# GpSimd writes ones on the diagonal of the residual's low part; the correction's product with the unit matrix goes

## What is computed

```python
def step(Sst, inp):
    q_t, k_t, v_t, g_t, beta_t = inp
    Sst = Sst * jnp.exp(g_t)[..., None, None]
    kv = jnp.einsum('bhk,bhkv->bhv', k_t, Sst)
    delta = (v_t - kv) * beta_t[..., None]
    Sst = Sst + k_t[..., None] * delta[:, :, None, :]
    o = jnp.einsum('bhk,bhkv->bhv', q_t, Sst)
    return (Sst, o)
```

## Time and profile before

| | |
|---|---|
| median of 3 runs | 1304.82 us (1302.67 to 1306.89) |
| the profiled execution | 1303.8 us, its span 1302.0 us |
| PE busy | 1200.0 us, 92% of the span |
| DVE busy | 1131.6 us, 87% |
| ACT busy | 975.0 us, 75% |
| POOL busy | 663.9 us, 51% |

### The profile page before, as it was taken

The page is one execution under the profiler, slowest core; times in us unless marked ns, Lnnn a source line. Parts: engine busy times, 40 slices in busy tenths (PEclk is TensorE's granted clock), DMA queues, the critical chain, the costliest instruction groups (busy, mean ns, idle before and its releaser), DMA issues.

```text
span 1302.0 us, 35596 instructions
## 1 busy us (share of the span) xinstructions
PE 1200.0 (92%) x13356; PEld 1008.6 (77%) x13356; DVE 1131.6 (87%) x2092; ACT 975.0 (75%) x2076; POOL 663.9 (51%) x566
## 2 busy tenths in 40 slices
...
GB/s 131 1 18 2 26 50 27 42 34 35 31 50 38 43 47 34 54 26 54 26 54 26 42 26 42 27 42 26 66 2 42 10 203 162 291 67 120 118 69 100
DMA packets 123893, 75.10 MB, mean 58 GB/s; under 512 B 93272, under 2 KB 116324, under 8 KB 122192
## 3 DMA queue, kind: packets, MB, share of 16 engines
...
...
## 4 chain that ended last, share of the span: by engine, by line
PE 79%; DVE 11%; issue 3%; ACT 2%; POOL 2%; DMA 2%; SPq 0%; POOLq 0%; DVEq 0%; ACTq 0%
PE bank L559 12%; PE bank L714 6%; PE bank L701 5%; PE bank L760 5%; PE bank L731 4%; PE bank L749 4%; PE bank L740 4%; PE bank L649 3%; PE bank L641 3%; PE bank L657 3%; DVE con L1056 2%; PE bank L609 2%; PE bank L610 2%; PE bank L1657 2%; PE bank L1682 2%
## 5 line engine op out<-in xcount | busy, mean ns | idle before, releaser
L1056 DVE SCALAR_TENSOR_TENSOR con<-bank,taps,con 128x1022 f32<-128x1022 f32 (+2 forms) x192 | 245.3, 1278 | 21.3 <-ACT con L829 16.7
L1214 POOL TENSOR_TENSOR gl<-const_sb,gc 128x512 f16<-128x512 f32 x128 | 130.0, 1043 | 120.7 <-DVE gc L1066 75.7
L559 PE MATMUL bank<-x,qkv 128*128 128x512 f16 x768 | 184.6, 392 | 6.4 <-DVE con L1056 6.3
L559 PEld LDWEIGHTS bank<-x,qkv 128*128 128x128 f16 x768 | 73.4, 100 | 89.1 <-issue 8.8
L1249 POOL TENSOR_TENSOR oo<-oo 128x512 f16<-128x512 f32 x64 | 76.1, 1199 | 121.8 <-ACT oo L959 121.8
L1114 DVE TENSOR_TENSOR X<-X,bank 128x512 f16<-128x512 f16 x160 | 108.8, 680 | 17.0 <-PE bank L649 15.7
L898 ACT ACTIVATE Z<-bank 128x512 f16<-128x512 f32 x160 | 96.4, 604 | 23.7 <-PE bank L657 23.7
L1105 DVE TENSOR_TENSOR Y<-bank,ymask 128x512 f16<-128x512 f32 x160 | 109.2, 683 | 2.9 <-PE bank L641 2.3
L829 ACT ACTIVATE con<-bank,taps 128x512 f32<-128x512 f32 x128 | 85.4, 687 | 33.1 <-PE bank L559 32.9
L1241 POOL TENSOR_TENSOR kd<-k_tok,gc 128x512 f32<-128x512 f32 x48 | 50.1, 1046 | 111.5 <-PE bank L740 111.5
L760 PE MATMUL bank<-out,sqo 128*128 128x256 f16 x768 | 96.2, 276 | 9.3 <-DMA sqo<-oo 9.2
...
## 6 DMA issues: line engine op xcount, KB each, us to landing
...
```

The costliest lines, as they stand in the source:

```text
L559: last = mm(bank[:, b], qkv16[:, w, a, t * P:(t + 1) * P], x16[:, x, a, b * S:(b + 1) * S], start=(a == k == 0), stop=(a == HT - 1 and k = ...
L1056: stt(out=out, in0=bank[:, 0:B, 0:S - k], scalar=taps[:, par, t, TAPS - 1 - k:TAPS - k], in1=out, op0=ALU.mult, op1=ALU.add).then_inc(tap_ ...
L1214: last = tt(gl[:, g % 2, k].rearrange("p (m r) d -> p m r d", m=2), upper.unsqueeze(1).unsqueeze(1).broadcast_to([P, 2, R, P]), gc[:, par, ...
```

## The change

`Z` loses its fourth product, the unit matrix with Z0 (L690: 4 matmuls a quarter, 16 a head, 256 in all). In its place the low part `res1` gets ones on its diagonal, so that the second product brings in Z0 as well. A new step `one` does that on GpSimd with an affine_select over a quarter (128x512, bf16, in place); it waits for DVE's `res1`, and `Z` on TensorE now waits for it (semaphore `res_low`). A quarter has one such step, so there are 64 more instructions on GpSimd.

```diff
         def finish_z(n, par, g):
 
-            is_free(pe, n, ("res", g), ("once", g), taking=("Z", g))
+            pe.wait_ge(res_low, 4 * n + g + 1)
+            is_free(pe, n, ("once", g), taking=("Z", g))
             out = take(n, "Z", g)
             for j in range(4):
                 u, at = 4 * g + j, slice(j * P, (j + 1) * P)
                 mm(out[:, at], res0[:, g, j], once[:, g % 2, j], start=True, stop=False)
                 mm(out[:, at], res1[:, g, j], Z0[:, u], start=False, stop=False)
-                mm(out[:, at], res0[:, g, j], Z0[:, u], start=False, stop=False)
-                last = mm(out[:, at], ident16[:], Z0[:, u], start=False, stop=True)
+                last = mm(out[:, at], res0[:, g, j], Z0[:, u], start=False, stop=True)
             filled(last, "Z", g)
...
+        def residual_one(n, par, g):
+            is_free(pool, n, ("res", g))
+            nc.gpsimd.affine_select(out=res1[:, g], in_=res1[:, g], pattern=[[0, 4], [1, P]], base=0,
+                                    channel_multiplier=-1, compare_op=ALU.not_equal, fill=1.0)\
+                .then_inc(res_low, 1)
...
-    (0, "solve", 0), (1, "gl", 3), (1, "aH", 1), (1, "decay", 2),
-    (0, "Z", 1), (1, "st", 0), (0, "su", 0), (1, "st", 1),
+    (0, "solve", 0), (0, "one", 1), (0, "one", 2), (1, "gl", 3),
+    (1, "aH", 1), (1, "decay", 2), (0, "Z", 1), (1, "st", 0),
```

More of the change, by code:

```diff
@@ L44 @@
     (0, "once", 1), (0, "res", 3), (1, "aH", 0), (1, "kk", 2),
[8 rows of a table removed]
-    (1, "aH", 3), (2, "load", "qkv"), (1, "turn", (0, 0)), (1, "unit", 3),
[10 rows of a table removed]
[L64 to L81, removed]
+    (0, "solve", 0), (0, "one", 1), (0, "one", 2), (1, "gl", 3),
[4 rows of a table added]
+    (1, "unit", 0), (0, "solve", 1), (0, "once", 3), (1, "p", (0, 0)),
+    (1, "unit", 1), (0, "qs", 1), (1, "st", 2), (1, "aL", 0),
+    (0, "su", 1), (1, "pT", 1), (1, "aL", 1), (1, "y", (1, 0)),
@@ new lines @@
+    (0, "pdl", 1), (1, "unit", 2), (0, "one", 3), (1, "aH", 3),
+    (2, "load", "qkv"), (1, "turn", (0, 0)), (1, "unit", 3), (1, "st", 3),
[10 rows of a table added]
+    (2, "proj", 1), (1, "p", (2, 1)), (1, "load", "out"), (1, "pT", 3),
+    (1, "y", (4, 0)), (0, "solve", 3), (1, "turn", (3, 0)), (2, "tap", 1),
+    (2, "gl", 2), (0, "power", 0), (2, "decay", 0), (1, "y", (3, 1)),
+    (0, "pdl", 3), (1, "p", (4, 0)), (0, "sum", 2), (0, "sum", 3),
+    (0, "sqo", 2), (0, "oT", 2), (2, "silu", 1), (0, "sqo", 3),
+    (1, "turn", (2, 1)), (1, "norm", 0), (2, "proj", 2), (1, "p", (3, 1)),
@@ new lines @@
+    (2, "tap", 2), (2, "sq1", 1), (0, "weigh", 0), (2, "tok", 0),
+    (2, "tok", 1), (1, "turn", (4, 0)), (0, "z", 0), (0, "z", 1),
+    (2, "silu", 2), (0, "high", 0), (0, "z", 2), (0, "low", 0),
+    (0, "low", 1), (0, "oT", 3), (1, "y", (4, 1)), (0, "weigh", 1),
+    (1, "turn", (3, 1)), (2, "proj", 3), (1, "p", (4, 1)), (0, "high", 1),
+    (2, "kT", 0), (0, "z", 3), (2, "kT", 1), (2, "v", (0, 1)),
+    (2, "tap", 3), (1, "turn", (4, 1)), (2, "silu", 3), (2, "v", (0, 0)),
+    (0, "weigh", 2), (0, "weigh", 3), (0, "high", 2), (1, "res", 0),
@@ L82 @@
+    (0, "high", 3), (0, "op", 0), (2, "proj", 0), (1, "once", 0),
+    (2, "tap", 0), (1, "res", 1), (0, "op", 1), (0, "low", 2),
+    (0, "low", 3), (1, "res", 2), (1, "Z", 0), (1, "once", 2),
+    (1, "one", 0), (1, "kd", 1), (2, "silu", 0), (1, "aL", 3),
     (0, "op", 2), (2, "decay", 1), (0, "op", 3),
@@ L136 @@
     (0, "y", (4, 1)), (1, "gl", 2), (1, "tok", 1), (0, "turn", (3, 1)),
[2 rows of a table removed]
+    (1, "proj", 3), (1, "v", (0, 1)), (0, "one", 0), (0, "one", 1),
+    (0, "one", 2), (1, "gl", 3), (0, "p", (4, 1)), (1, "v", (0, 0)),
+    (1, "tap", 3), (0, "one", 3), (1, "pT", 0), (1, "unit", 0),
     (1, "unit", 1), (0, "turn", (4, 0)), (1, "pT", 1), (0, "res", 0),
@@ L180 @@
     (1, "load", "z"), (1, "once", 2), (0, "op", 2), (2, "silu", 0),
-    (2, "decay", 1), (0, "low", 3), (0, "oT", 3), (1, "kd", 1),
-    (0, "op", 3), (1, "pT", 3),
+    (2, "decay", 1), (0, "low", 3), (0, "oT", 3), (1, "one", 0),
+    (1, "kd", 1), (0, "op", 3), (1, "pT", 3),
 ]
 LAST = [
-    (15, "load", "qkv"), (14, "kk", 0), (14, "gl", 3), (14, "load", "out"),
-    (14, "aT", 0), (13, "Z", 2), (14, "kk", 1), (13, "split", "out"),
-    (13, "once", 1), (14, "aT", 1), (13, "res", 3), (13, "solve", 0),
[19 rows of a table removed]
@@ L208 @@
-    (15, "gc", 0), (14, "turn", (1, 1)), (15, "proj", 1), (13, "sum", 1),
[3 rows of a table removed]
[L212 to L217, removed]
@@ L218 @@
-    (13, "high", 0), (15, "silu", 2), (13, "weigh", 1), (15, "tap", 3),
[4 rows of a table removed]
[L223 to L226, removed]
+    (15, "load", "qkv"), (14, "kk", 0), (13, "one", 1), (13, "one", 2),
+    (14, "gl", 3), (14, "load", "out"), (14, "aT", 0), (13, "Z", 2),
@@ new lines @@
+    (14, "kk", 1), (13, "split", "out"), (13, "once", 1), (14, "aT", 1),
+    (13, "res", 3), (13, "solve", 0), (14, "kk", 2), (13, "split", "z"),
[16 rows of a table added]
+    (13, "su", 2), (13, "pdl", 2), (13, "sqo", 2), (14, "load", "z"),
+    (14, "p", (1, 1)), (14, "y", (3, 0)), (14, "turn", (2, 0)), (13, "ks", 3),
+    (13, "qs", 3), (14, "y", (2, 1)), (14, "p", (3, 0)), (15, "gc", 0),
+    (14, "turn", (1, 1)), (15, "proj", 1), (13, "sum", 1), (15, "gl", 0),
+    (14, "aL", 3), (13, "sum", 2), (14, "y", (4, 0)), (14, "p", (2, 1)),
@@ new lines @@
+    (15, "load", "out"), (14, "oT", 0), (14, "kd", 1), (13, "solve", 3),
+    (15, "gl", 1), (15, "tap", 1), (14, "oT", 1), (14, "turn", (3, 0)),
+    (15, "decay", 0), (14, "turn", (2, 1)), (13, "pdl", 3), (15, "silu", 1),
+    (13, "sqo", 3), (14, "norm", 0), (14, "p", (4, 0)), (14, "y", (3, 1)),
+    (15, "proj", 2), (14, "oT", 2), (13, "power", 0), (13, "sum", 3),
+    (14, "p", (3, 1)), (15, "tap", 2), (15, "sq1", 1), (14, "oT", 3),
+    (13, "weigh", 0), (15, "tok", 0), (15, "tok", 1), (14, "turn", (3, 1)),
@@ L227 @@
+    (13, "z", 0), (14, "y", (4, 1)), (13, "z", 1), (13, "high", 0),
+    (15, "silu", 2), (13, "weigh", 1), (15, "tap", 3), (15, "load", "z"),
[4 rows of a table added]
+    (13, "low", 1), (13, "high", 2), (14, "once", 0), (15, "tap", 0),
+    (13, "low", 2), (15, "proj", 0), (13, "high", 3), (15, "silu", 3),
+    (13, "op", 1), (14, "res", 1), (14, "res", 2), (14, "turn", (4, 1)),
+    (14, "Z", 0), (14, "one", 0), (13, "low", 3), (14, "once", 2),
     (13, "op", 2), (15, "silu", 0), (15, "decay", 1), (15, "kk", 0),
@@ L236 @@
     (15, "st", 2), (14, "su", 1), (15, "y", (1, 0)), (15, "turn", (0, 0)),
[9 rows of a table removed]
-    (15, "unit", 1), (14, "solve", 3), (14, "sum", 1), (15, "p", (2, 1)),
-    (15, "aL", 0), (15, "turn", (3, 0)), (15, "y", (4, 0)), (14, "sqo", 2),
-    (14, "sqo", 3), (14, "pdl", 3), (15, "aL", 1), (15, "turn", (2, 1)),
[4 rows of a table removed]
-    (14, "high", 1), (15, "norm", 0), (15, "y", (4, 1)), (15, "turn", (3, 1)),
-    (14, "weigh", 2), (15, "res", 0), (15, "res", 1), (15, "p", (4, 1)),
-    (15, "once", 0), (14, "high", 2), (15, "unit", 3), (14, "z", 3),
@@ L256 @@
-    (15, "Z", 0), (14, "weigh", 3), (14, "high", 3), (14, "op", 0),
-    (15, "aL", 2), (15, "once", 1), (15, "turn", (4, 1)), (15, "res", 2),
[3 rows of a table removed]
-    (15, "sum", 0), (15, "Z", 1), (15, "solve", 1), (15, "sqo", 0),
-    (14, "power", 0), (14, "low", 0), (15, "qs", 1), (15, "su", 1),
-    (15, "pdl", 1), (15, "once", 3), (14, "low", 1), (15, "oT", 3),
[5 rows of a table removed]
-    (15, "sum", 2), (15, "solve", 3), (15, "sqo", 3), (15, "pdl", 3),
-    (15, "sum", 3), (15, "weigh", 0), (15, "z", 0), (15, "z", 1),
-    (15, "high", 0), (15, "z", 2), (15, "weigh", 1), (15, "high", 1),
@@ L272 @@
-    (15, "high", 2), (15, "z", 3), (15, "power", 0), (15, "weigh", 2),
-    (15, "low", 0), (15, "high", 3), (15, "low", 1), (15, "weigh", 3),
-    (15, "op", 0), (15, "low", 2), (15, "op", 1), (15, "op", 2),
-    (15, "op", 3), (15, "low", 3),
[9 rows of a table added]
+    (14, "sum", 0), (14, "qs", 3), (15, "unit", 1), (14, "solve", 3),
+    (14, "sum", 1), (15, "p", (2, 1)), (15, "aL", 0), (15, "turn", (3, 0)),
+    (15, "y", (4, 0)), (14, "sqo", 2), (14, "sqo", 3), (14, "pdl", 3),
+    (15, "aL", 1), (14, "one", 3), (15, "turn", (2, 1)), (15, "sq", 0),
@@ new lines @@
+    (14, "sum", 2), (14, "z", 0), (15, "unit", 2), (14, "sum", 3),
+    (15, "oT", 2), (15, "y", (3, 1)), (15, "p", (4, 0)), (14, "z", 1),
+    (15, "p", (3, 1)), (15, "turn", (4, 0)), (14, "weigh", 0), (15, "v", (1, 0)),
+    (14, "weigh", 1), (14, "high", 0), (14, "z", 2), (14, "high", 1),
+    (15, "norm", 0), (15, "y", (4, 1)), (15, "turn", (3, 1)), (14, "weigh", 2),
+    (15, "res", 0), (15, "res", 1), (15, "p", (4, 1)), (15, "once", 0),
+    (14, "high", 2), (15, "unit", 3), (14, "z", 3), (15, "Z", 0),
@@ new lines @@
+    (14, "weigh", 3), (14, "high", 3), (14, "op", 0), (15, "aL", 2),
+    (15, "once", 1), (15, "turn", (4, 1)), (15, "res", 2), (14, "op", 1),
[4 rows of a table added]
```

(6 more changed lines are left out.)

30 lines of the change are left out of this document (19 added, 11 removed), and 114 rows, old and new, of tables (FIRST, LAST, ORDER).

## The result

The changed kernel takes 1308.7 us (median of 12 runs, 1302.9 to 1310.2), the kernel before on the same chip 1304.85 (12 runs). The ratio is 1.0026, 95% interval 1.0015 to 1.0036: slower by about 3.4 us. The forecast was 1309.5, in a range of 1300 to 1313, with chances of 0.44 for slower, 0.40 for within 0.3% and 0.16 for faster. The interval leaves out a change of nothing, but 0.26% lies inside the 0.3% that the forecast had set, so of these three it was the middle one that came.

A forecast was written before the change was run, and what follows sets the result against it. The prediction took a loop of TensorE and DVE work in each head as the bound, not TensorE alone. Terms of 4.4 - 0.65 + 1.0 = +4.7 us gave 1309.5 us against 1304.8, range 1300 to 1313.

The forecast's parts named there:

- The bound: Middle heads: TensorE waits 0.28 us for DVE at `st`, so only `Z` 3's 0.22 of 0.90 us saved counts.
- DVE's part: DVE's stretch of a head from `tap` 0 to `res1` of quarter 3; forecast to grow by 0.56 us.
- `one` by itself: The new GpSimd step: 0.60 us, bounds 0.3 and 0.85; no `Z` of the middle waits, so no cost by itself.
- the ring: A head's two-part loop: TensorE from `st` to the next head's `proj` 0, DVE from `tap` 0 to `res1` 3.
- `gl` onto `aT`: Middle heads: `one` 2 pushes `gl` 3 onto the first `aT`, 0.56 us later; a head costs +0.34 us.
- The three last heads: End of the run: +0.34 us at head 13, -0.45 at head 14, +1.0 at the turn to head 15.
- the same turn at head 13: Head 13 was taken to turn like the 12 middle windows, at +0.34 us.
- head 14: Turns outside the middle's pattern; gains between nothing and 0.9 us, taken as -0.45.
- the turn to 15: Turn to head 15, through `weigh` 3 on DVE: +1.2 us from sharing with GpSimd, -0.2 for `Z` 2, +1.0 together.
- the hold: GpSimd's second `gl`, reading SBUF, keeps DVE's first `aT` waiting until it ends: 0.56 us in each middle head.
- The sum: Whole kernel: 4.4 - 0.65 + 1.0 = +4.7 us, giving 1309.5 us against 1304.8.
- the term of the middle: Middle heads: 0.56 - 0.22 = +0.34 us each; with head 13 counted in, 13 x 0.34 = +4.4 us.

The follow-up runs named there:

- the fills that read nothing: Changed kernel with the two products of `gl` 3 replaced by GpSimd fills of the same tile, made twice, reading no SBUF: 1299.9 us, one run.
- The halves: Two runs: changed kernel with the unit-matrix product back and a select that never fires, 1312.3 us; kernel before without that product and nothing in its place, 1298.5 us.
- the select only: Changed kernel with the unit-matrix product put back and a select that never fires, writing nothing new: 1312.3 us, ratio 1.0049 to the kernel before.

## Why the prediction was right

**The bound.** Right. TensorE's 0.28 us at `st` were a wait for DVE under ACT's name; of 0.90 us of products a head got 0.23 back (forecast 0.22), by the run without them. TensorE's rest beside DVE's part turned into the wait at `st`, 1.27 us instead of the 1.5 forecast. Most of the missing 0.24 us were spent further up beside DVE's part: TensorE, ahead since the shorter `Z` 0, now waits for ACT at `once`, which costs nothing in this kernel, as it would have waited at `st` anyway. The timeline of the weight loads shows it; before, there was no such wait:

```profile
616.14 0.23 PEld L684 LDWEIGHTS bank<-Z,res 128*128 128x128 f16 x4 [0.19 <-ACT res L908]
```

**`one` by itself.** Right: 0.63 to 0.65 us, and in the changed kernel no `Z` of the middle waits for one. Behind `gl` it costs nothing measurable while the ring is closed (63.66 with and without it), and by the starts of `Z` 2 some 0.2 us a head once the ring is open. Forecast 0.60, bounds 0.3 and 0.85.

**`gl` onto `aT`.** Right in place and size: 1.25 us, DVE's part longer by 0.56, a head by 0.33 (forecast 0.34). The rule of the Trainium skill (SBUF — State Buffer, "Who interferes with whom") was the support for `gl` doing this beyond the rows of `pT` and `unit`, as no row of before had `gl` beside such an instruction. That the holder keeps the ports for the whole instruction the section says beside DVE's two-port modes; for a DVE instruction with two SBUF inputs it states the contention with a GpSimd read, and that issue order decides. The trace agrees now, from both sides: the reading `gl` held `aT` until 0.14 us before its reported end, the fills that read nothing did not, and DVE's ops with one input in PSUM kept 0.68 us beside all of them.

**The three last heads.** Here the working failed, and this is the term that the total hides. The step was "and the same turn at head 13", with -0.45 for head 14 and +1.0 for the turn to 15: together +0.9 us. Measured: -0.26, -1.07 and +0.79, together -0.54.
- Head 13 isn't the same turn. The table of the end has `Z` 2 ahead of `kk` 1, so DVE idled 0.42 us ahead of its second `kkm` in the kernel before; the shorter `Z` 0 and 2 count there, and the hold falls in part into that idle time. The halves show both: without the product the turn is 0.52 us shorter (62.78), and the select costs 0.05 us beside the products (63.35 against 63.30) and 0.26 without them (63.04 against 62.78). That `Z` 2 sits on that path is shown by the 0.83 us that the later `one` 2 cost.
- Head 14 is 59.87 in the kernel before, and 58.79 with the product gone, 58.80 with the change: all of the products' work counts there and `one` costs nothing. I had taken half. That it is 1.07 and not 0.90 comes from a wait of TensorE's `op` for the DMA that turns the output, 0.21 us in the kernel before and none in these two. The two other kernels with the products have it too, 0.53 us with the `z` split later (60.17) and 0.70 us with the select only (60.35). Less that wait all three take 59.64 to 59.66 us, 0.86 more than 58.79. From the timeline of PE before:

```profile
995.27 1.48 PE L760 MATMUL bank<-out,sqo 128*128 128x256 f16 x12 [0.21 <-DMA sqo<-oo]
```

- The turn to 15: `weigh` took 3.12 us instead of the 2.14 of its timeline row in the kernel before (2.06 in the chain), +1.0 where +1.2 was forecast. By the halves the select costs this turn 1.24 us (44.80) and the products give 0.45 back (43.11), where +1.2 and -0.2 were forecast. `one` 0 also made `Z` 0 wait 0.76 us, which I had not seen, but it isn't what the turn lost: TensorE then stands idle another 1.52 us for DVE's `y` behind `weigh`, where it was 1.04. DVE's, then PE's timeline:

```profile
1049.19 3.12 DVE L1180 SCALAR_TENSOR_TENSOR oo<-oo,rso,zs 128x128 f32<-128x128 f32 x4
```
```profile
1048.92 0.23 PE L694 MATMUL bank<-once,res 128*128 128x128 f16 x1 [0.76 <-POOL res L1244]
...
1053.05 0.22 PE L673 MATMUL bank<-X,aH 128*128 128x128 f16 x1 [1.52 <-DVE y L1190]
```

**The sum.** Eleven heads at +0.33, the one from the first `power` to the second at +0.14 and the last three at -0.54 make +3.2 us; the measured ratio gives +3.4. The forecast was +4.7, 1.4 of it too much in the last three heads; the -0.2 in it for head 0 can't be told from the spread of the start. The median lies 3.85 over that of before, 0.8 under the forecast; beside the spread of the experts' stretch this difference tells nothing. So the mechanism and the term of the middle were right, and the total came out nearer than its parts by some luck. In the profiled execution of the kernel before four of the heads are 0.07 to 0.70 us longer than 63.89, which none of the changed one is. In three of them TensorE falls behind at `op`, which waits for the DMA that turns the output (0.55 us at 295.18, in the head of 64.59); the rest of it shows further on, at `Z` 3, and what it waits for there the profile doesn't say.
